# Two-layer sequence model: the routed experts' gate and up columns in three products instead of four, the combine weights' loads moved ahead of the blocks' end

## What is computed

```python
cw = _combine_weights(xt, gate_w)          # top 4 of 16 experts, within 2 of 4 groups
for e in range(16):
    g, u = jnp.split(xt @ expert_up_w[e].T, 2, axis=-1)     # 256 -> 2 x 176
    out = out + cw[:, e:e + 1] * ((silu(g) * u) @ expert_down_w[e].T)   # 176 -> 256
out = out + _swiglu(xt @ shared_up_w.T) @ shared_down_w.T   # shared width 352
```

## Time and profile before

| | us |
|---|---|
| three runs | 1626.9, 1620.39, 1627.39 |
| their median | 1626.9 |
| profiled execution, its own time | 1621.94 |
| span of that execution, first to last instruction | 1619.9 |

### The profile page before, as it was taken

The page is one execution under the profiler, slowest core; times in us unless marked ns, Lnnn a source line. Parts: engine busy times, 40 slices in busy tenths (PEclk is TensorE's granted clock), DMA queues, the critical chain, the costliest instruction groups (busy, mean ns, idle before and its releaser), DMA issues.

```text
span 1619.9 us, 29536 instructions
## 1 busy us (share of the span) xinstructions
PE 1519.8 (94%) x9685; PEld 1334.4 (82%) x9685; DVE 1101.4 (68%) x2967; ACT 736.1 (45%) x1905; POOL 504.0 (31%) x354
## 2 busy tenths in 40 slices
PE   7999999999999989999999999999996799999887
PEld 5988888898988877887888888888884689998776
DVE  5878778787878775556578669777865444321687
ACT  5666666666666553433623433353322533343221
POOL 2323222232323002432355235635743022000550
PEclk9999999999999999999999999999998799999999
DMA  8564646465563105656675567657654487797774
GB/s 274 199 234 161 238 149 236 140 245 187 197 234 136 44 1 191 195 184 200 192 247 174 168 190 223 192 169 223 195 177 144 153 296 246 238 283 247 248 241 147
DMA packets 131943, 317.44 MB, mean 196 GB/s; under 512 B 15653, under 2 KB 41421, under 8 KB 130813
## 3 DMA queue, kind: packets, MB, share of 16 engines
q1 hardware_dynamic: 127229, 303.50, 57.4%
q0 software_dynamic: 4608, 12.59, 2.3%
HBM read 226.90 MB, written 88.60 MB: 195 GB/s over the span
## 4 chain that ended last, share of the span: by engine, by line
PE 53%; issue 17%; DVE 14%; POOL 8%; ACT 5%; another core or an unknown queue 1%; DMA 0%; DVEq 0%; ACTq 0%; POOLq 0%; SPq 0%
PE psum L505 46%; POOL act_sb L830 4%; POOL mix L848 3%; PE psum L1724 2%; POOL xs L860 1%; DVE s_sb L1308 1%; PE psum L1735 1%; ACT p_sb L962 1%; PE psum L1960 1%; PE psum L1714 1%; ACT kT_hi L921 1%; PE psum L1929 1%; DVE s_sb L1306 1%; DVE kT_lo L1190 1%
## 5 line engine op out<-in xcount | busy, mean ns | idle before, releaser
L505 PE MATMUL psum<-xT_hi,gu_w 128*128 128x512 f32 x1088 | 373.5, 403 | 20.5 <-DVE act_sb L1456 8.6
L830 POOL TENSOR_TENSOR act_sb<-act_sb,comb 128x512 f32<-128x512 f32 x96 | 159.5, 1661 | 373.4 <-DVE act_sb L1456 373.4
L505 PEld LDWEIGHTS psum<-xT_hi,gu_w 128*128 128x128 f32 x1088 | 205.8, 189 | 74.4 <-issue 20.0
L1003 ACT ACTIVATE gated<-psum 128x512 f32<-128x512 f32 (+1 forms) x138 | 82.6, 598 | 387.3 <-PE psum L505 352.1
L1456 DVE TENSOR_TENSOR act_sb<-psum,gated 128x512 f32<-128x512 f32 (+1 forms) x138 | 95.0, 688 | 187.5 <-PE psum L505 156.7
L505 PE MATMUL psum<-xT_lo,gu_w 128*128 128x512 f32 x544 | 215.8, 397 | 0.0
L786 POOL TENSOR_TENSOR split_stage<-raw_stage,split_stage 128x768 fp32r<-128x768 f32 x56 | 103.1, 1842 | 352.4 <-ACT split_stage L911 352.4
L505 PEld LDWEIGHTS psum<-d_w,act_hi 128*128 128x128 f32 (+1 forms) x1104 | 149.6, 188 | 13.1 <-issue 1.5
L505 PE MATMUL psum<-d_w,act_hi 128*128 128x256 f32 (+1 forms) x1104 | 154.4, 282 | 0.0
L960 ACT ACTIVATE p_sb<-s_sb,neg_max 128x128 f32<-128x128 f32 x128 | 51.5, 403 | 171.7 <-DVE neg_max L1308 171.7
L505 PE MATMUL psum<-xbT,bw 128*88 128x128 f32 x1008 | 122.8, 276 | 1.5 <-ACT xbT L1075 1.3
(11 more groups left out here) (253 smaller groups left out, 3993.1 us busy)
## 6 DMA issues: line engine op xcount, KB each, us to landing
gu_w<-w_split SPq DMA_DIRECT2D x138, 512.0 KB
w_split<-split_stage SPq DMA_DIRECT2D x56, 768.0 KB, 4.0
d_w<-w_split SPq DMA_DIRECT2D x138, 256.0 KB
bw<-l_w SPq DMA_DIRECT2D x63, 480.0 KB
xs<-zeros SPq DMA_DIRECT2D x21, 1280.0 KB, 7.5
raw_stage<-w_all SPq DMA_DIRECT2D x56, 384.0 KB, 4.5
decay_all<-decay_dram SPq DMA_DIRECT2D x32, 384.0 KB, 4.9
in_w<-w_split SPq DMA_DIRECT2D x40, 256.0 KB
```

The lines of the kernel that those rows point to most:

```text
L505: last = nc.tensor.matmul(out_ap, w, m, start=start and n == 0, stop=stop and n == len(pairs) - 1, **kw)
L830: pool.tensor_tensor(act_sb[:, s % 2, :], act_sb[:, s % 2, :], comb[:, comb_block(s) % 2, :], ALU.mult).then_inc(comb_done, 1)
L1003: act.activation(gated[to, s % 2, :], psum[0:to.stop - to.start, G_BANK, :], ACT.Silu).then_inc(gated_ready, 1)
```

## The change

It has four parts.

1. **Three pieces.** Gate's first 128 columns are a piece, up's first 128 another. The last 48 columns of gate (`REST`) and of up share the third: gate at columns 0 to 47, zeros to 63, up at 64 to 111. So gate and up of a block are 6 products, four with 128 weight columns and two with 112. In `bw` a partition has 992 values. Silu and the product with up become two instructions each, of 128x128 and 48x128; the second silu reads partitions 0 to 47 and writes 64 to 111. Down has 128 rows in its first product and 112 in its second, of which the first 64 are zeros (two memsets, of bw_last on POOL at the program's start, of b_act on DVE at block 0); `bw_last` is loaded with 48 rows.
2. **b_out moves** into space between the rings of bw, away from `comb`, and the wait for all blocks' stores ahead of the last layer's `comb_load` goes.
3. **Both halves of the last layer's combine weights** are issued at tick `K0 - 4` = 180.
4. **Ticks of the slots.** The fourth pair's slots from 7 on are spread over 56 blocks instead of 48. A few of the third pair's last slots (49, 55 to 57) stand one tick later.

```diff
@@ -151,14 +151,18 @@
...
 WIDTH = L1["width"]
-PIECE = WIDTH // 2
 BLOCK = 128
...
 LAST_ROW = SLOT * REGION + (SPARE - 1) * BLOCK
-UP = 2 * WIDTH
+
+
+REST = WIDTH - P
+UP = 2 * P + HALF + REST
+PIECES = (0, P), (P, 2 * P), (2 * P, UP)
+LAST_ROWS = slice(HALF, HALF + REST)
 BW = DC * UP + D
@@ -213,8 +217,8 @@
...
 MARKS = (NORM, 28), (0, 33), (9, 41), (28, 54), (34, 58), (43, 66), (62, 80), (68, 84), (70, 85), (75, 90), (77, 91), (96, 103), (104, 107), (106, 108), (109, 109), (113, 110), \
-    (115, 111), (118, 112), (120, 113), (122, 114), (FRONT[-1] + END, 115)
-LAST_MARKS = (NORM, 110), (-5, 110), (-4, 113), (-3, 114), (-1, 115), (2, 116), (6, 120), (7, B0), (END, B0 + 48)
+    (115, 111), (117, 112), (120, 113), (122, 114), (123, 115), (FRONT[-1] + END, 116)
+LAST_MARKS = (NORM, 110), (-5, 110), (-4, 113), (-3, 114), (-1, 115), (2, 116), (6, 120), (7, B0), (END, B0 + 56)
@@ -291,7 +295,7 @@
...
         const_ready = sem("const_ready")
-        ZEROS, TABLES, SENTINELS = 5, 11, 14
+        ZEROS, TABLES, SENTINELS = 5, 12, 15
@@ -366,6 +370,10 @@
...
         bw = nc.alloc_sbuf_tensor_at("bw", [P, BW_RING, T], F32, offset=xT_at)
+
+        assert OUT_RING == BW_RING and BW <= 2 * BANK
+        b_outs = nc.alloc_sbuf_tensor_at("b_out", [P, OUT_RING, T], F32, offset=xT_at)
+        b_out = b_outs[:, :, 2 * BANK:2 * BANK + D]
         og = nc.alloc_sbuf_tensor_at("og", [P, UNITS_IN, T], F32, offset=xT_at)
@@ -377,7 +385,6 @@
...
         zeros = nc.alloc_sbuf_tensor_at("zeros", [P, 1, BANK], F32, offset=high.at)
-        b_out = nc.alloc_sbuf_tensor_at("b_out", [P, OUT_RING, D], F32, offset=high.at)
         comb = high("comb", [P, 2, BANK])
@@ -521,11 +528,11 @@
...
-            at = c * UP + i * PIECE
-            return bw[:, n % BW_RING, at:at + PIECE]
+            a, b = PIECES[i]
+            return bw[:, n % BW_RING, c * UP + a:c * UP + b]
         def down_w(n, i):
-            return bw_last[0:PIECE, n % BW_RING, :] if i else bw[0:PIECE, n % BW_RING, DC * UP:BW]
+            return bw_last[0:HALF + REST, n % BW_RING, :] if i else bw[:, n % BW_RING, DC * UP:BW]
@@ -635,8 +642,6 @@
...
                     sp.wait_ge(comb_done, combed(COMBS[k - 2][4]))
-                if k == QUADS * L0["combs"]:
-                    blocks_stored(sp)
                 sp.wait_ge(comb_stored, 16 * (turn_no(f, q) + 1))
@@ -691,7 +696,7 @@
...
                 sp.dma_start(bw[:, n % BW_RING, 0:BW], w[:, 0:BW]).then_inc(bw_loaded[n % BW_RING], 16)
-                sp.dma_start(bw_last[0:PIECE, n % BW_RING, :], w[0:PIECE, BW:BW + D]).then_inc(bw_loaded[n % BW_RING], 16)
+                sp.dma_start(bw_last[LAST_ROWS, n % BW_RING, :], w[LAST_ROWS, BW:BW + D]).then_inc(bw_loaded[n % BW_RING], 16)
@@ -749,7 +754,7 @@
...
                 for k, (f, _, m, s0, _) in enumerate(COMBS):
-                    if s == s0 - 2:
+                    if i == K0 - 4 if f is L1 else s == s0 - 2:
                         comb_load(k)
@@ -800,6 +805,8 @@
...
                 low_part(0, part)
+
+            pool.memset(bw_last[0:HALF], 0.0).then_inc(const_ready, 1)
             pool.memset(prefix[:], 0.0).then_inc(const_ready, 1)
@@ -1075,10 +1082,10 @@
...
             def block_gate(n):
-                h = slice(0, PIECE)
                 act.wait_ge(gu_ready, n + 1)
                 wait(act, bt_ready, n - 1)
-                act.activation(b_gated[h, n % 2, :], psum[h, gu_bank(n), 0:2 * BLOCK], ACT.Silu).then_inc(b_gated_ready, 1)
+                act.activation(b_gated[:, n % 2, 0:BLOCK], psum[:, gu_bank(n), 0:BLOCK], ACT.Silu)
+                act.activation(b_gated[LAST_ROWS, n % 2, BLOCK:2 * BLOCK], psum[0:REST, gu_bank(n), 2 * BLOCK:3 * BLOCK], ACT.Silu).then_inc(b_gated_ready, 1)
@@ -1434,10 +1441,11 @@
...
             def block_act(n):
-                h = slice(0, PIECE)
                 dve.wait_ge(b_gated_ready, n + 1)
                 wait(dve, b_down_done, n - 1)
-                dve.tensor_tensor(b_act[h, n % 2, :], psum[h, gu_bank(n), 2 * BLOCK:4 * BLOCK], b_gated[h, n % 2, :], ALU.mult).then_inc(bt_ready, 1)
+                dve.tensor_tensor(b_act[:, n % 2, 0:BLOCK], psum[:, gu_bank(n), BLOCK:2 * BLOCK], b_gated[:, n % 2, 0:BLOCK], ALU.mult)
+                dve.tensor_tensor(b_act[LAST_ROWS, n % 2, BLOCK:2 * BLOCK], psum[LAST_ROWS, gu_bank(n), 2 * BLOCK:3 * BLOCK],
+                                  b_gated[LAST_ROWS, n % 2, BLOCK:2 * BLOCK], ALU.mult).then_inc(bt_ready, 1)
@@ -1560,6 +1568,7 @@
...
                     add_down(BREAK - 1)
+                    dve.memset(b_act[0:HALF, :, BLOCK:2 * BLOCK], 0.0)
                     block_act(0)
@@ -1964,14 +1973,14 @@
...
                 wait(pe, bt_ready, n - 1)
-                for i in range(4):
-                    last = chain(psum[0:PIECE, gu_bank(n), i * P:(i + 1) * P], [(up_w(n, c, i), xbT[:, n % 2, c, :]) for c in range(DC)])
+                for i, (a, b) in enumerate(PIECES):
+                    last = chain(psum[0:b - a, gu_bank(n), i * P:(i + 1) * P], [(up_w(n, c, i), xbT[:, n % 2, c, :]) for c in range(DC)])
                 last.then_inc(gu_ready, 1)
...
                 wait(pe, b_copied, n)
-                chain(psum[:, DOWN_BANK, 0:D], [(b_act[0:PIECE, n % 2, i * BLOCK:(i + 1) * BLOCK], down_w(n, i)) for i in range(2)]) \
+                chain(psum[:, DOWN_BANK, 0:D], [(b_act[0:(P, HALF + REST)[i], n % 2, i * BLOCK:(i + 1) * BLOCK], down_w(n, i)) for i in range(2)]) \
                     .then_inc(b_down_done, 1)
@@ -2135,9 +2144,14 @@
...
     l1_w = np.zeros((-(-LAST_ROW // REGION) + 1, P, BW + D), x.dtype)
-    l1_w[:SLOT, :, :DC * UP] = up.reshape(SLOT, DC, P, UP).transpose(0, 2, 1, 3).reshape(SLOT, P, -1)
+    gate_up = np.zeros((SLOT, D, UP), x.dtype)
+    for i, half in enumerate((up[:, :, :w], up[:, :, w:])):
+        gate_up[:, :, i * P:(i + 1) * P] = half[:, :, :P]
+        gate_up[:, :, 2 * P + i * HALF:2 * P + i * HALF + REST] = half[:, :, P:]
+    l1_w[:SLOT, :, :DC * UP] = gate_up.reshape(SLOT, DC, P, UP).transpose(0, 2, 1, 3).reshape(SLOT, P, -1)
     down = a["L1_ffn_expert_down_w"].transpose(0, 2, 1)
-    l1_w[:SLOT, :PIECE, DC * UP:] = down.reshape(SLOT, 2, PIECE, D).transpose(0, 2, 1, 3).reshape(SLOT, PIECE, -1)
+    l1_w[:SLOT, :, DC * UP:BW] = down[:, :P]
+    l1_w[:SLOT, LAST_ROWS, BW:] = down[:, P:]
     rows = lambda w: w.reshape(DC, P, -1).transpose(1, 0, 2)
```

## The result

The changed kernel took 1600.41 us (median of 4 runs, 1599.27 to 1601.74), the kernel before 1624.73 us beside it (4 runs, 1620.39 to 1627.39): ratio 0.9851, 95% interval [0.983, 0.9873]. Timed twice more, in two later sessions, it gave 1604.25 us (0.9889 [0.987, 0.9908]) and 1599.25 us (0.985 [0.9829, 0.9871]). So the gain is 18 to 26 us, 1.1 to 1.6%. The profiled execution went from a span of 1619.9 us to 1597.1: 22.8 us.

What follows compares the result with a forecast made beforehand. The prediction took PE's own work to bound the blocks, with the DMA engines close behind. Terms -24, +7, +1.5 and -0.5 summed to -16 us, 1606 from the profiled execution; 2 added for run spread gave 1608, range 1595 to 1620.

Steps and rivals of the forecast that it cites:

- Gate and up, -24: Block stage on PE: 16 records become 12, saving 0.38 us a block, 24 us for 63 blocks (19 to 27.5).
- The 116 ns: Gate and up: assumed time of each of the 8 records with 128 weight columns, between bounds of 110 and 120.
- The weights' transfer, +7: Plain blocks: weights come late, period 2.70 instead of 2.45 us in 28 blocks, 7 us given back (0 to 14).
- L: Block weights: time from first issue to landing of the second transfer, taken as 5.2 us in plain blocks, setting the period.
- ScalarE and VectorE, 0: Blocks: the added instructions stay covered, a path of 1.1 us plus hand-overs against 2.45; cost 0, uncovered 19 us.
- The fourth pair over 56 blocks, 0: Block stage: PE work moved, not changed, so cost 0, bounds -2.6 to +4 us.
- The way into the blocks, 0 (-2 to +1): Ahead of the blocks: read of block rows moves; ScalarE's 16.04 us idle covers PE's possible gain or loss.
- Combine weights and the dense steps, +1.5 and -0.5: Behind the blocks: sixteen early loads delay stores and last copy, +1.5 us; fewer issues ahead of gu_w loads, -0.5.
- the stall of the earlier trace: Behind the blocks: PE's 4.75 us before 1509, expected to stay; 6 us in all if it went.
- A: Blocks: rival that transfers stay hidden and PE sets every block, -24 to -27.5, 1592 to 1601 us; chance 0.20.
- B: Blocks: rival that DMA engines bound nearly all, period 2.75, -5 to -10, 1613 to 1621 us; chance 0.16.
- C: Blocks: rival that the closer rhythm lengthens weight landing, period 3.35 in plain blocks, +12, 1636 us; chance 0.06.

Runs made afterwards that it cites:

- light_weights: Changed kernel with the fifth and later loads of a block's gate, up and first down columns bringing 64 of 128 rows: 1599.46 us, ratio 0.9846.
- one_gate: Changed kernel without the second gating instruction of ScalarE and second product of VectorE per block (48 hidden rows left out): 1601.03 us, ratio 0.9857.
- slots48: Changed kernel with the fourth pair over 48 blocks and the two marks ahead of the blocks as before: 1605.27 us, ratio 0.9894.
- last48: Changed kernel with the fourth pair over 48 blocks, but the two new marks ahead of the blocks kept: 1601.39 us, ratio 0.9871.
- comb_late: Changed kernel with the combine weights loaded in the dense steps as before, behind the blocks' stores: 1598.85 us, ratio 0.9859.
- changed_again: The changed kernel unaltered, timed and profiled a second time in a later session: 1604.25 us, ratio 0.9889.
- changed_third: The changed kernel unaltered, timed and profiled a third time in a later session: 1599.25 us, ratio 0.985.

## Why the prediction was right, and where it was not

**Gate and up, -24.** Right in mechanism, a little small: the twelve records take 1.33 us, nearest to my 1.31 for 109 ns, so 0.41 us a block and 26 in all. The 116 ns that the prediction took for the 8 records were too many: they take 112. The long row of 256-column products at 120 ns was the wrong neighbour; the two 128x128 products at 110 were the right one. The Trainium skill ("TensorE: Matmul & The Clock Gate", LDWEIGHTS) gives a load its columns over 1.2 GHz, 107 ns for 128, which would just hide behind 109; the trace agrees but for 3 ns a record.

**The weights' transfer, +7.** The mechanism is shown, by the landings and by light_weights. In size: records alone would have made the blocks 216.7 - 25.8 = 190.9 us; they take 197.2, 199.6 and 197.6, so 6.3 to 8.7 us are given back, and some 1.3 us more in the last two profiles, whose clock rose sooner. But my 7 was for weights alone. The profile calls 3.7, 6.2 and 5.2 us of it new idle time of PE; of that, ahead of gate and up, 1.6, 5.1 and 3.1 us. Idle time understates a wait, since a record's modelled end lies 0.17 us behind the next start in a steady row. By the distances between starts, worked out from the traces from the third block on, the waits ahead of gate and up are 5.5, 10.4 and 7.3 us against 2.3 before, and those ahead of down 3.7, 2.5 and 3.3 against 1.5. So this term is 3.2 to 8.1 us, 5.4 in the mean: 7 was a fair size for it. That it also comes near the 6.3 of the first profile, which has other waits in it, is luck. It doesn't come as a period of 2.70 in 28 plain blocks: plain blocks take 2.42, and 12, 17 and 12 of the 63 blocks wait ahead of gate and up (4 before), with up to 1.4 us of idle time each. L, from the first issue to the second landing, was near enough: in the kernel after, bw_last lands a median of 5.1 us after its issue in 1403:1420 and 4.2 us in 1440:1460 (of the few whose landing the trace has), and is issued 0.5 us behind bw, so 5.6 and 4.7, with 5.2 between.

```profile
bw_last<-l_w SPq DMA_DIRECT2D x6, 48.0 KB, 5.1
...
bw_last<-l_w SPq DMA_DIRECT2D x8, 48.0 KB, 4.2
```

What failed is to take one L for every block: single landings of bw_last took 4.4 to 5.3 us in the eight waits above, and a formula with one L gives all or nothing.

**ScalarE and VectorE, 0.** Right for the plain block (2.42 us, and one_gate's time), wrong in one place: 0.7 to 1.7 us more idle time ahead of down than before (1.0 to 2.1 by starts), most of it behind VectorE's choice of experts. I had the margin of 2.45 against 1.1 us from blocks in which VectorE has nothing else to do, and didn't look at the longest chain that stands ahead of a block's product.

**The fourth pair over 56 blocks, 0.** Within its bounds; not told from nothing.

**The way into the blocks, 0 (-2 to +1): the step that failed.** It brought 3.4 to 4.3 us in the three profiles, outside the bounds. I had costed the row that moved, the read of first_row, and not what the marks do to the other instructions of these ticks, and I had reasoned that ScalarE's 16 us of idle time cover any shift. The instruction behind that idle time did move. In the order of time on ACT of the kernel after:

```profile
1248.70 0.78 ACT L1049 ACTIVATE conv<-psum,cols 128x512 f32<-128x512 f32 x1 [10.73 <-remote]
```

It starts 6.4 us sooner than at 1255.1. But it isn't what the way in hangs on: in the eleven profiles with the new marks it starts 46.9 to 51.9 us behind the second quad's scatters, and the way in is 72.6 to 73.6 all the same. What moved with the way in is elsewhere. The steps up to the third quad's scatter became 1.5 to 2 us shorter. And of PE's last two waits for VectorE's conv ahead of the first turn, before and after:

```profile
1258.28 0.79 PE L505 MATMUL psum<-xT_hi,in_w 128*128 128x512 f32 x1 [7.24 <-DVE conv L1505]
1265.44 0.50 PE L505 MATMUL psum<-xT_hi,in_w 128*128 128x512 f32 x1 [1.90 <-DVE conv L1505]
```

```profile
1259.13 0.80 PE L512 MATMUL psum<-xT_hi,in_w 128*128 128x512 f32 x1 [4.33 <-DVE conv L1513]
1263.68 0.80 PE L512 MATMUL psum<-xT_hi,in_w 128*128 128x512 f32 x1 [1.62 <-DVE conv L1513]
```

the second stood 7.2 us behind the first and stands 4.6 behind it now: twelve products of the fourth pair's projections stood between them, and six do now, the other six having gone ahead of the first wait. That the marks do it is shown by slots48 and last48; which of these steps carries how much was not tried apart.

**Combine weights and the dense steps, +1.5 and -0.5.** The stores left at 1468.5, the last copy waited 1.6 us longer, as said; the stall of the earlier trace rows stayed, as said. The time shows neither term: from the first dense product to the end it was 1.8 to 2.9 us shorter, where my two terms say 1 us longer, and comb_late, without the early loads, was shorter still. What makes it shorter stays open.

**The sum** by measured terms, for the first profile: -25.8 in gate and up, +6.3 in the blocks' waits, -3.4 ahead of them, -1.8 behind, and +1.9 up to the end of the second quad's scatters, which was 0 and -0.3 in the two other profiles: -22.8. Kernel before and after have the same clock at the start of the blocks there, so it doesn't enter. The forecast's -16 lacks the way in (3.4 us) and what came behind the blocks (2.8), and has the records 2 us short. Of the rivals, A gave the right number (1592 to 1601) by a wrong reason: transfers do not stay hidden. B and C are out: plain blocks of 2.42 us exist throughout.

## What to carry to other kernels

Where a bottleneck engine gets a seventh shorter, look for what is now late in the *worst* block, not in the median one: here a transfer with a median just in time cost 3 to 8 us, and one chain of small instructions on an idle engine up to 1.4 us. See too what the wait's semaphore counts: here it held gate and up for a transfer that they don't read. When ticks of a list move, go through every engine's instructions of these ticks, not only the one that the move was for. And before a part of a change is called worth 3 us, time and profile the same kernel twice, and compare the granted clock of the stretches: here its time differed by 5 us with itself, and one stretch by 2.7 us at half clock.

## What the runs showed of the hardware that I had not expected

- The end of the second quad's scatters, far ahead of the blocks, comes at 1195.9 to 1196.2 us in three profiles (the kernel before, changed_again, changed_third) and at 1198.1 to 1201.3 in the eleven others. The two groups part at one wait of PE near 585 us: 0.84 or 0.85 us in the three, 2.4 in the eleven, far ahead of any changed step. It is 1.6 us of the difference between two profiles of one kernel; what sets it isn't known. In the kernel after:

```profile
586.01 0.87 PE L1733 MATMUL psum<-ident,p_sb 128*128 128x128 f32 x3 [2.42 <-DVE pT_lo L1330]
```

- Twelve products in a row with 112 columns of weights each cost PE the same as with 88, 109 ns from start to start, and with 128 columns 3 ns more (a moving side of 128 columns in all three).
- With the DMA engines at 0.85 or 0.86 of their time over the blocks and at 0.86 to 0.89 in 1320:1464, PE's waits ahead of gate and up differed between profiles of one kernel by a factor of two (3.1 to 6.6 us).
- TensorE went on 0.09 us after the last transfer that it waited for had landed, in eight of eight waits whose landing the trace has.
